# Two output planes in place of four in a mixture-of-experts stage that adds its results by scatter

## What is computed

```
x = x + 0.5 * ffn(layernorm(x))        # mixture of experts, 64 experts
x = x + attention(layernorm(x))        # linear attention, 16 heads
x = x + 0.5 * ffn(layernorm(x))        # the same mixture of experts again
```

```
y = zeros.at[tok].add(contrib * weight)     # one token can be hit by up to 6 experts
return y + silu(x ws1) * (x ws3) @ ws2
```

## Time and profile before

| | |
|---|---|
| median of three runs | 616.61 us |
| span of the profiled execution | 615.3 us (what lies around it is about 1.3 us of the median) |
| busy in the span | PE 448.7, DVE 356.6, POOL 333.6, PEld 298.5, ACT 223.2 us |
| mean granted TensorE clock | 0.726 of full speed |
| first expert stage, first to last scatter | 103.25 to 182.41 us |
| second expert stage, first to last scatter | 494.00 to 573.14 us |

### The profile page before, as it was taken

How to read it: one execution, slowest core, us unless ns; L and a number is a source line. 1 busy time by engine, 2 the same in 40 slices (tenths; PEclk the granted TensorE clock), 3 DMA queues, 4 the chain that set the end, 5 groups by cost and what they waited for, 6 DMA issues and landing times.

```text
span 615.3 us, 12760 instructions
## 1 busy us (share of the span) xinstructions
PE 448.7 (73%) x4788; PEld 298.5 (49%) x4788; DVE 356.6 (58%) x992; ACT 223.2 (36%) x509; POOL 333.6 (54%) x259
## 2 busy tenths in 40 slices
PE   1876965996699425799999979147877399957970
PEld 1823643553345313577777768146445255524440
DVE  6497981221113992687777865487999232212097
ACT  4732112332224268555555530184321133312420
POOL 6177786888886700322222220003877678888691
PEclk9987785555559755799999986558778555555995
DMA  7988500101008990001111110541000000100592
GB/s 256 387 243 317 230 8 7 11 5 11 6 5 314 410 368 1 1 3 38 35 34 35 34 36 10 161 173 52 2 0 8 8 8 6 10 6 7 166 410 108
DMA packets 34388, 60.39 MB, mean 98 GB/s; under 512 B 12611, under 2 KB 18846, under 8 KB 33870
## 3 DMA queue, kind: packets, MB, share of 16 engines
q1 hardware_dynamic: 23078, 58.41, 26.5%
q0 software_dynamic: 11264, 1.38, 2.5%
HBM read 37.43 MB, written 29.36 MB: 109 GB/s over the span
## 4 chain that ended last, share of the span: by engine, by line
PE 32%; DVE 30%; DMA 12%; issue 12%; ACT 7%; POOL 4%; another core or an unknown queue 1%; SPq 1%; DVEq 0%; POOLq 0%; ACTq 0%
DVE X L971 9%; DMA rows_d<-A 5%; PE bank L776 5%; PE bank L895 5%; PE bank L793 4%; PE bank L876 4%; PE bank L766 3%; PE bank L786 3%; ACT A L508 3%; DMA planes_d<-Bb,put_i 3%; DVE Cb L1074 2%; DVE bn L976 2%; DMA Bb<-planes_d 2%; POOL planes_d L438 2%; DVE A L1055 2%
## 5 line engine op out<-in xcount | busy, mean ns | idle before, releaser
L438 POOL DMA_INDIRECT planes_d<-Bb,put_i x64 | 100.4, 1569 | 26.1 <-issue 19.4
L452 POOL DMA_INDIRECT A<-rows_d,tok_i x64 | 71.4, 1116 | 20.1 <-issue 16.6
L1104 DVE TENSOR_TENSOR ring<-ring,bank 128x88 f32<-128x88 f32 x64 | 15.8, 246 | 107.2 <-ACT ring L574 77.4
L673 PE MATMUL bank<-ident,A 128*128 128x128 f32 x96 | 21.6, 399 | 54.4 <-ACT A L508 40.2
L479 POOL TENSOR_TENSOR Bb<-Cb,chm 128x576 f32<-128x576 f32 x16 | 19.0, 1221 | 67.1 <-DVE Cb L1138 33.7
L396 POOL TENSOR_TENSOR Bb<-Eb,st 128x512 f32<-128x512 f32 x8 | 8.9, 1112 | 79.3 <-DVE st L1022 79.3
L766 PE MATMUL bank<-ident,A 128*128 128x128 f32 x64 | 29.8, 465 | 29.4 <-DMA A<-rows_d,tok_i 23.5
L703 PE MATMUL bank<-XT,ws1s 128*88 128x512 f32 x64 | 41.4, 734 | 6.2 <-DVE Eb L1016 5.3
L568 ACT ACTIVATE ring<-bank 128x128 f32<-128x128 f32 x64 | 17.8, 278 | 77.6 <-PE bank L766 67.0
L673 PEld LDWEIGHTS bank<-ident,A 128*128 128x128 f32 x96 | 17.4, 212 | 57.3 <-issue 29.9
L479 POOL TENSOR_TENSOR Bb<-w3s,chm 128x576 f32<-128x576 f32 x16 | 17.9, 1148 | 49.2 <-PE bank L918 49.2
(11 more groups left out here) (155 smaller groups left out, 1108.3 us busy)
## 6 DMA issues: line engine op xcount, KB each, us to landing
planes_d<-zeros SPq DMA_DIRECT2D x8, 2048.0 KB, 20.9
w3s<-in_w3T SPq DMA_DIRECT2D x2, 2816.0 KB
rows_d<-A SPq DMA_DIRECT2D x8, 512.0 KB, 12.4
A<-planes_d SPq DMA_DIRECT2D x8, 512.0 KB, 9.5
PL<-planes_d SPq DMA_DIRECT2D x8, 512.0 KB, 10.2
Cb<-planes_d SPq DMA_DIRECT2D x8, 512.0 KB, 10.9
Bb<-planes_d SPq DMA_DIRECT2D x8, 512.0 KB, 12.0
w1s<-in_w1T SPq DMA_DIRECT2D x1, 2816.0 KB
```

The lines of the kernel that those rows point to most:

```text
L438: pool.indirect_dma_start(out=planes_d[f], in_=Y[:, s, :], in_offset=None, out_offset=bass.IndirectOffsetOnAxis(ap=put_i[:, s:s + 1], axis=0),
L452: pool.indirect_dma_start(out=A[:, t, :], out_offset=None, in_=rows_d, in_offset=bass.IndirectOffsetOnAxis(ap=tok_i[:, t:t + 1], axis=0), ...
L673: ins = pe.transpose(bank[g % 2][:, (i % 4) * P:(i % 4 + 1) * P], A[:, i, :], ident[:, :])
```

## The change

It halves the planes. Every slab now uses plane 0 for its first half and plane 1 for its second, so a scatter waits for the one just before it, by one semaphore `added`. The planes cleared and loaded are two for each f in place of four, DVE adds two planes for each quarter, and POOL adds none. The lead of the gathers becomes a constant: `ahead = min(NS, s + 7)`, so 7 gathers go ahead of the first scatter, and one more ahead of each of the scatters 1 to 25.

```diff
-    LEAD = (16, 6)
+    LEAD = 7
+    NPL = 2
...
-        planes_d = [nc.dram_tensor(f"planes{f}_d", (4 * T, D), F32, kind="Internal").ap() for f in range(2)]
+        planes_d = [nc.dram_tensor(f"planes{f}_d", (NPL * T, D), F32, kind="Internal").ap() for f in range(2)]
...
-        added = [sem(f"added{k}") for k in range(2)]
+        added = sem("added")
...
-        PLANES = (A_flat, PL[:, :], Cb[:, 0:T], Bb[:, 0:T])
+        PLANES = (A_flat, PL[:, :])
...
-                for k in range(4):
+                for k in range(NPL):
                     dst = planes_d[f][k * T:(k + 1) * T, :].rearrange("(p a i) d -> p a (i d)", p=P, i=4)
                     sp.dma_start(dst, zeros[:, :].unsqueeze(1).broadcast_to([P, NI // 4, 4 * D])).then_inc(planes_zero, 16)
...
-                for k in range(2):
-                    sp.wait_ge(added[k], 16 * (NS // 2) * (f + 1))
+                sp.wait_ge(added, 16 * NS * (f + 1))
...
-                count(plane0[k * CAP:(k + 1) * CAP, :], k * T, [[0, NS // 2], [2 * T, 2]], 0)
+                count(plane0[k * CAP:(k + 1) * CAP, :], k * T, [[0, NS]], 0)
...
                     if s == 0:
-                        pool.wait_ge(planes_zero, 16 * 4 * (f + 1))
+                        pool.wait_ge(planes_zero, 16 * NPL * (f + 1))
                     pool.wait_ge(y_sb, f * NS + s + 1)
-                    n = f * (NS // 2) + s // 2
-                    if n:
-                        pool.wait_ge(added[s % 2], 16 * n)
+                    if f or s:
+                        pool.wait_ge(added, 16 * (f * NS + s))
                     pool.indirect_dma_start(out=planes_d[f], in_=Y[:, s, :], in_offset=None,
                                             out_offset=bass.IndirectOffsetOnAxis(ap=put_i[:, s:s + 1], axis=0),
-                                            bounds_check=4 * T - 1, oob_is_err=False,
-                                            compute_op=ALU.add).then_inc(added[s % 2], 16)
+                                            bounds_check=NPL * T - 1, oob_is_err=False,
+                                            compute_op=ALU.add).then_inc(added, 16)
...
-                    ahead = min(NS, s + 1 + max(LEAD[1], LEAD[0] - s // 2))
+                    ahead = min(NS, s + LEAD)
...
-                def add_planes(g):
-
-                    cols = slice(g * GI * D, (g + 1) * GI * D)
-                    pool.wait_ge(part_in[g], 16 + 64 * (f + 1))
-                    pool.tensor_tensor(out=PLANES[2][:, cols], in0=PLANES[2][:, cols], in1=PLANES[3][:, cols],
-                                       op=ALU.add).then_inc(planes_added, 1)
-
                 for g in range(EARLY, NSH):
-                    if g >= NSH - 2:
-                        add_planes(g - (NSH - 2))
                     shared_gates(g)
-                for g in range(2, NG):
-                    add_planes(g)
...
-                    dve.wait_ge(part_in[g], 16 + 64 * (1 + n // 2))
-                    for buf in PLANES[0:3]:
-                        if buf is PLANES[2]:
-                            dve.wait_ge(planes_added, NG * (n // 2) + g + 1)
+                    dve.wait_ge(part_in[g], 16 + 16 * NPL * (1 + n // 2))
+                    for buf in PLANES:
                         then(dve.tensor_tensor(xg, xg, buf[:, cols], ALU.add))
```

More of the change, by code:

```diff
@@ L227, in macaron_kernel @@
         z_added = sem("z_added")
-        planes_added = sem("planes_added")
         out_done = sem("out_done")
@@ L337, in _ @@
             sp.wait_ge(out_done, 16 * NG)
-            sp.wait_ge(planes_zero, 16 * 8)
+            sp.wait_ge(planes_zero, 16 * 2 * NPL)
         @block.gpsimd
```

## The result

The changed kernel takes 657.62 us (median of four runs, 655.85 to 658.86), the kernel before 616.14 us in the same comparison. The ratio is 1.065, with a 95% interval of 1.062 to 1.068: 41.5 us slower. The spans of the profiled executions differ by 657.1 - 615.3 = 41.8 us.

What follows compares the result with a forecast made beforehand. Expert stages were taken as bound by POOL making descriptors, with the new wait exposing landing and wake-up. 615.3 + 76.0 (scatters) - 25.6 (after the stages) = 665.7 us of span, so 667 us; range 644 to 700.

Steps and rivals of the forecast that it cites:

- the likeliest case: Whole kernel: the forecast itself, 667 us, own range 653 to 690, chance 0.60.
- The step: Scatter to scatter on POOL: 3.78 us, 31 steps 117.2 us against 79.16, +38.0 a stage, +76.0 for both.
- The two terms: In each scatter step: landing, POOL's start to semaphore, 2.9 us; wake-up, sequencer issuing after the wait, 0.88 us.
- The gather inside the landing: Between scatters: each gather runs inside the landing, so ten moved gathers cost nothing while a step exceeds 3.26 us.
- the wake-up is hidden: Rival at scatter waits: DMA starts at once after the gather, 25 steps of 3.26 us, 631 us in all; chance 0.09.
- The first scatter does not come earlier.: Stage start: POOL is ready some 13 us sooner, but slab 0's result is due at 102.37 regardless; no gain.
- The third rival: Stage start: the gather burst causes ACT's stalls; a lead of 7 saves about 9 us a stage, 649 us; chance 0.13.
- The part behind the stage: After the last scatter: fewer plane loads and additions, earlier shared expert; gain 12.8 us for each f, 25.6 together.
- the gates: POOL's shared gates without add_planes before them: group 7 complete 23.7 us after the last scatter's start (T), not 28.7.
- Clearing half as much: Plane clearing: four transfers of 2 MB fewer, in the shadow of other work with nobody waiting; nothing gained.
- The rival of slow landings: Scatter landings: each costs 3.27 us plus 0.88 wake-up, shared expert no earlier; 701 us; chance 0.14.
- The estimate by the Trainium skill: Scatter step by the page's fixed DMA cost: 1.56 + 2.0 + 0.88 = 4.44 us, whole about 708 us.

Runs made afterwards that it cites:

- the first comparison: The changed kernel against the kernel before, on a chip not on record: 657.62 us against 616.14, ratio 1.065.
- the kernel where nothing else changes: The kernel before with only planes 0 and 1 loaded and added, POOL adding none, odd slabs' results left out: 586.01 us, ratio 0.960.
- Without rows: The changed kernel with the bound of the scatter's row indices set to 0, so nearly every row is skipped: 645.56 us against 656.48.

## Why the prediction was right, and where it was off

The forecast was 667 us, slower; measured are 657.6, inside the range of 644 to 700 and inside the likeliest case's own 653 to 690. The sign and the mechanism were right, and the experiment with the wait alone shows the mechanism by itself: +78 us with nothing else changed. The sizes of the terms were off, against each other: in the span of the first comparison the scatters cost 5.8 us more than forecast and the part behind them gained 4.5 us less, while the start of the stages gained 17.8 us where nothing was forecast. That 667 is only 9 us above the result owes as much to this as to the sum, and 5.5 of the 17.8 us are what the two stages of that one trace of the kernel before had too much.

**The step.** Forecast 3.78 us, +76.0 for both stages; measured 3.86 and 3.89, +81.8. The two terms were the right ones: landings on the chain of 2.7 to 4.2 us where 2.9 was taken, and a wake-up of 0.81 where 0.88 was read from the first scatter. What I did not know is that landings depend on rows: 2.7 is that of a scatter with few or none. I took the spread for chance. The single long steps, up to 5.18 us, lie outside the 3.60 to 4.15 that I gave.

**The gather inside the landing.** The prediction said that it costs nothing. Nothing can be seen of a cost on average: with 15 gathers between the scatters the step is 3.84 and 3.82 us (the wait alone), with 25 it is 3.86 and 3.89, and 3.89 and 3.84. But it sets a floor. The chain of the kernel after:

```profile
107.40 0.88 POOL A L450
108.28 0.04 issue
108.32 0.03 POOLq L436
...
109.08 1.59 POOL planes_d L436
```

The sequencer passes to the next scatter only when the gather has run for 0.9 us, and the scatter starts 0.76 after its move. The gather starts 1.90 us after its scatter, so that is 1.90 + 0.92 + 0.76 = 3.58 us; the smallest step with a gather is 3.57, without one 3.50. This floor lies only 0.07 us above a short landing with its wake-up, 2.70 + 0.81. Without rows the smallest steps are 3.50 with a gather and 3.43 without. So the rival "the wake-up is hidden" (3.26) fails at just this: the wake-up comes behind the gather too.

**"The first scatter does not come earlier."** This step failed. I took 102.37, when slab 0's result was ready in the trace of before, as given. It held two stalls of ACT that the kernel before does not have on another chip, where this result is ready at 91.25. The second limit, the burst itself, is in the rows shown: the 3.07 us of idle time in front of the scatter at 103.25 put the end of the burst at 100.18. So even without the stalls a lead of 17 holds the first scatter to about 98.3, and a lead of 7 frees it. The short burst is worth 13.0 us of the two stages on one chip, and in the first comparison, with the stalls in the trace of before, 17.8. The third rival gave this sum (18 us, 649 us) with the wrong cause: the stalls are not made by the burst. The term was put at nothing; with 13 us in its place the forecast would have been 654.

**The part behind the stage.** Forecast -12.8 for each, measured -10.1 and -11.0. The working was right for the gates; in the kernel where nothing else changes, group 7 starts its write at T + 23.3 and T + 22.4, and 23.1 was forecast (T + 23.7 at its end, less 0.6). What was left out is that PE is later in the kernel after, by 1.3 and 2.5 us, as its rows show with its clock at the lower level after the wait for POOL. For f = 0 that is half of what is missing: the end was forecast at T + 44.3, it is T + 45.7 where only two planes are loaded and T + 47.0 in the kernel after. The other half is in ACT's work behind group 7, 21.8 us in both kernels where 20.6 was added up. Clearing half as much cost or gave nothing to be seen: from the last copies of f = 0 to the first gather of f = 1 it takes 226.3 us before and 226.4 after, and the first gather of f = 0 is at 76.02 and 74.91.

**The rival of slow landings** (701 us) is out: with many rows in every slab it would be nearer, at 4.1 us a step by the median of those slabs.

The estimate by the Trainium skill, "DMA: Bandwidth & Descriptors", section on the anatomy of one DMA (2.0 us fixed, so a step of 4.44 us and 708 us), is too high for most of these scatters: from the end of POOL's work to the landing it is 1.2 us for the one at 618.90 (618.90 + 1.55 to 621.64). By the medians, a scatter with tens of rows takes about half a microsecond more, still below the page's figure; the one at 151.12, with a landing of 3.90 us, takes 2.3 and is above it. The page counts the setup into its 2.0 us, and the estimate added POOL's 1.56 to it. Counted from POOL's start, no landing on the chain of the kernel after is below 2.69 us, so read in that way the page's figure is too low.

## What to carry to other kernels

A chain of dependent scatters costs the landing plus the wake-up of the issuing sequencer, here 3.5 to 4.1 us a link in most steps, against 1.87 us of descriptor work. One slab of room between a scatter and its dependent hid nearly all of it (79.16 us a stage, of which 31 x 1.87 + 15 x 1.39 = 78.8 are POOL's own work); with none, only a gather fits in. So count what the extra planes cost (here 21 to 24 us for two) against links x (step - occupancy). And before a date in a trace is called a limit, ask what stood in front of it: take the same program's trace again, and look for the next limit behind it. Look also whether the named end of a wait is the event that the wait needed; here DVE was named for 12 of the 31 scatters behind the first of a stage, and its result for slab 5 had lain there for 8 us.

## What the runs showed that was not expected

- Of the kernels that compute the whole layer the best is the one before with POOL's own additions moved to DVE, 602.9 us against 610.0. DVE's addition took up to 5.69 us beside POOL's instructions and 1.22 alone.
- A step was some 0.5 us longer behind a scatter with tens of rows than behind one with almost none (4.06 and 3.60 us), while POOL's own part was 1.55 to 1.59 us with rows and without.
- One program's trace held two unexplained stalls of ACT in each expert stage, which its trace from another chip did not have; the stretches that held them are 5.5 us longer, of 7.4 us between the two spans.
